# Masked keys on GpSimd: four pieces behind both products instead of two around one

## What is computed

```python
qkv = win @ qkv_w + qkv_b
q, k, v = jnp.split(qkv, 3, axis=-1)
q = to_heads(q) * dh ** (-0.5)
attn = jnp.einsum('bhnd,bhmd->bhnm', q, k)
attn = attn + bias                      # and the mask of shifted windows
attn = jax.nn.softmax(attn, axis=-1)
out = jnp.einsum('bhnm,bhmd->bhnd', attn, v)
out = out @ proj_w + proj_b
```

## Time and profile before

| | |
|---|---|
| median of 3 runs | 8296.84 us (8291.62 to 8297.04) |
| the profiled execution | 8299.7 us, of which the span of the trace is 8298.0 us |
| TensorE's matmuls busy | 94% of the span |
| ScalarE, VectorE busy | 75%, 73% |
| GpSimd busy | 43% |
| mean granted TensorE clock | 0.976 of full speed |

### The profile page before, as it was taken

The page is one execution under the profiler, slowest core; times in us unless marked ns, Lnnn a source line. Parts: engine busy times, 40 slices in busy tenths (PEclk is TensorE's granted clock), DMA queues, the critical chain, the costliest instruction groups (busy, mean ns, idle before and its releaser), DMA issues.

```text
span 8298.0 us, 213285 instructions
## 1 busy us (share of the span) xinstructions
PE 7781.9 (94%) x76732; PEld 4632.0 (56%) x76732; DVE 6095.1 (73%) x12339; ACT 6242.5 (75%) x11905; POOL 3585.1 (43%) x2453
## 2 busy tenths in 40 slices
PE   6899999999999999999999999999999999999997
PEld 4655555555555555555555555555555555555554
DVE  6377777777777777777777777777777777777774
ACT  0288878887888888778878878888787888787781
POOL 4244444444444444444444444444444444444440
PEclk9999999999999999999999999999999999999996
DMA  7000000000000000000000000000000000000006
GB/s 218 9 20 20 19 19 19 19 21 19 19 19 19 21 18 19 19 20 19 19 19 20 19 19 19 19 20 19 21 19 19 19 21 19 19 19 21 19 16 205
DMA packets 286131, 236.84 MB, mean 29 GB/s; under 512 B 41564, under 2 KB 280670, under 8 KB 284766
## 3 DMA queue, kind: packets, MB, share of 16 engines
q1 hardware_dynamic: 240944, 179.42, 8.1%
q10 hardware_dynamic: 35886, 19.97, 0.8%
q0 software_dynamic: 8192, 22.49, 0.8%
HBM read 112.56 MB, written 109.18 MB: 27 GB/s over the span
## 4 chain that ended last, share of the span: by engine, by line
issue 53%; POOL 30%; PE 10%; ACT 3%; DMA 3%; DVE 1%; POOLq 1%; SPq 0%; ACTq 0%; DVEq 0%
POOL E L411 19%; POOL Kbd L420 11%; PE bank L867 1%; PE bank L900 1%; DMA cm<-xT 1%; DMA xT<-cm 1%; PE bank L885 1%; PE bank L926 1%; PE bank L957 1%; PE bank L848 1%; PE bank L849 1%; PE bank L1017 1%; PE bank L943 1%; ACT E L472 0%; PE bank L962 0%
## 5 line engine op out<-in xcount | busy, mean ns | idle before, releaser
L411 POOL TENSOR_TENSOR E<-E,rs 113x588 f32<-113x588 f32 x1536 | 1819.2, 1184 | 3379.0 <-DVE rs L701 3379.0
L670 DVE TENSOR_TENSOR S<-bank,bias 113x294 f32<-113x294 f32 x3072 | 1412.5, 460 | 1428.9 <-PE bank L885 1364.8
L420 POOL TENSOR_TENSOR Kbd<-KT,headmask 112x1176 f32<-112x1176 f32 x768 | 1701.8, 2216 | 1042.6 <-ACT KT L478 1042.6
L867 PE MATMUL bank<-ident,E 113*113 113x113 f32 x9216 | 1620.3, 285 | 289.1 <-ACT ET L446 160.4
L867 PEld LDWEIGHTS bank<-ident,E 113*113 113x113 f32 x9216 | 1232.6, 180 | 1086.5 <-issue 540.8
L446 ACT ACTIVATE ET<-bank 113x339 f32<-113x339 f32 x3072 | 1367.7, 445 | 489.2 <-PE bank L867 471.3
L900 PEld LDWEIGHTS bank<-ET,V 113*48 113x48 f32 x36864 | 1005.5, 126 | 781.5 <-ACT ET L446 485.5
L695 DVE TENSOR_REDUCE sm<-E 113x12 f32<-113x588 f32 x1536 | 1163.8, 758 | 328.2 <-ACT E L472 328.2
L678 DVE TENSOR_REDUCE mx<-S 113x12 f32<-113x588 f32 x1536 | 1172.2, 763 | 39.6
L684 DVE TENSOR_TENSOR S<-S,mx 113x588 f32<-113x588 f32 x1536 | 1168.5, 761 | 0.0
L900 PE MATMUL bank<-ET,V 113*48 113x49 f32 x36864 | 1152.5, 212 | 10.3 <-issue 9.8
(11 more groups left out here) (88 smaller groups left out, 9136.9 us busy)
## 6 DMA issues: line engine op xcount, KB each, us to landing
xin<-xT SPq DMA_DIRECT2D x384, 98.0 KB, 2.0
xT<-xout SPq DMA_DIRECT2D x384, 98.0 KB, 1.8
xin<-xT SPq DMA_DIRECT2D x384, 73.5 KB, 2.0
xT<-xout SPq DMA_DIRECT2D x384, 73.5 KB, 1.8
xT<-cm POOLq DMA_DIRECT2D x128, 171.5 KB, 3.6
cm<-xT SPq DMA_DIRECT2D x128, 171.5 KB, 3.6
tm<-in_x SPq DMA_DIRECT2D x128, 147.0 KB
out<-tm ACTq DMA_DIRECT2D x128, 147.0 KB
```

What stands on the lines that cost most here:

```text
L411: pool.tensor_tensor(e, e, r, ALU.mult).then_inc(norm_done, 1)
L420: pool.tensor_tensor(Kbd[:, j.mod(2), p0:p0 + P // 2], k, m, ALU.mult).then_inc(kbd_done, 1)
L670: dve.tensor_tensor(strided(S[:, p, 0, 0:1], [[1, HN]]), pS[p % 2][0:M2, 0:HN], bi, ALU.add)\
L867: last = pe.transpose(pT[0:M2, k * M2:(k + 1) * M2], strided(E[:, j.mod(2), p, 2 * k, 0:1], [[1, M2]]), ident[0:M2, 0:M2])
```

## The change

GpSimd now makes Kbd in four pieces of two windows (112 x 588 elements each) instead of two of four windows (112 x 1176), and all of them after product 1. `kbd_done` rises four times a step. TensorE waits for the piece of each pair of windows instead of for a half at p = 0 and p = 4. ScalarE waits, before it overwrites KT, for the last piece of the step before.

```diff
-            def spread_k(j, half):
-
-                if half == 0:
+            def spread_k(j, quarter):
+
+                if quarter == 0:
                     pool.wait_ge(kT_done, gv(j, 1, 1))
-                p0 = half * P // 2
-                k = strided(KT[:, p0, 0:1], [[N, P // 2], [0, HEADS], [1, N]])
-                m = strided(headmask[:, 0:1], [[0, P // 2], [1, HEADS], [0, N]])
-                pool.tensor_tensor(Kbd[:, j.mod(2), p0:p0 + P // 2], k, m, ALU.mult).then_inc(kbd_done, 1)
+                p0 = 2 * quarter
+                k = strided(KT[:, p0, 0:1], [[N, 2], [0, HEADS], [1, N]])
+                m = strided(headmask[:, 0:1], [[0, 2], [1, HEADS], [0, N]])
+                pool.tensor_tensor(Kbd[:, j.mod(2), p0:p0 + 2], k, m, ALU.mult).then_inc(kbd_done, 1)
...
                 if b:
                     norm(b, 0)
-                if a:
-                    spread_k(a, 0)
                 if b:
                     norm(b, 1)
                 if a:
-                    spread_k(a, 1)
+                    for quarter in range(4):
+                        spread_k(a, quarter)
...
                 act.wait_ge(k_mm, gv(j, 1, 1))
+                if not j.before(1):
+                    act.wait_ge(kbd_done, gv(j, 4, 0))
                 act.activation(flat(KT), pA0[0:R, 0:TOK], ACT.Identity, bias=cols[:, t, BK:BK + 1]).then_inc(kT_done, 1)
...
-                if p % (P // 2) == 0:
-                    pe.wait_ge(kbd_done, gv(j, 2, 1 + 2 * p // P))
+                pe.wait_ge(kbd_done, gv(j, 4, 1 + p // 2))
```

## The result

| | before | changed |
|---|---|---|
| median of 9 runs | 8298.36 us (8291.62 to 8306.60) | 8321.85 us (8317.10 to 8327.99) |
| the profiled execution, its span | 8299.7 us, 8298.0 us | 8319.77 us, 8318.1 us |
| mean granted TensorE clock | 0.976 | 0.973 |

The ratio is 1.0028 [1.0017, 1.0038]: slower by 23.5 us. That is above the 0.2% that I had called measurable and outside my range, which ended at 8318.

What follows compares the result with a forecast made beforehand. The prediction took alternating ScalarE and TensorE stretches, a 19.68 us step repeated 384 times, to bound the kernel. Its five terms were all 0, giving 8297 us, no change, with a range of 8278 to 8318 us.

Steps and rivals of the forecast that it cites:

- The bound: ScalarE's and TensorE's stretches close the 19.68 us step, repeated 384 times; POOL and VectorE matter only if late.
- Part 1: On POOL, product 1 goes ahead of the keys and starts 1.79 us earlier; nobody waits for it: worth 0.
- Part 2: On POOL, four key pieces replace two halves at 1.14 us each; the last ends 0.64 us later.
- Part 3: TensorE's need for the pieces: piece 0 is 1.68 us in time, the others are asked for later: worth 0.
- Part 4: POOL-VectorE port: last piece overlaps the subtraction 0.08 us, 0.13 is free, 0.41 more spare: worth 0, upper end 1344 us.
- Rival 1: POOL-VectorE port wait outgrows the slack: 154 us slower per 0.1 us a piece above 1.255 us; chance 0.10.
- Part 5: Added kbd_done waits on TensorE and ScalarE, and ScalarE's register instruction, are already fulfilled or hidden: 0.
- The sum: All five terms are 0, so the whole kernel was forecast at 8297 us, no change.
- rival 3: TensorE's loop-pass ends, 6.0 or 4.7 us each, shift with the code: -27 to +27 us; chance 0.10, half slower.
- Rivals 2 and 4: TensorE waits for POOL: up to 173 us faster, chance 0.05; ScalarE's register instruction delays its path: +12 to +31 us, 0.03.

## Why the prediction was wrong, by its own steps

- **The bound** (ScalarE's and TensorE's stretches, POOL and VectorE in neither): right. Only a GpSimd operation that overlaps VectorE's subtraction by 0.72 us, where the change makes it 0.09 (medians), moved the period.
- **Part 1** (product 1 earlier, worth 0): right, it starts 0.08 us after its reciprocal, and no stop of TensorE got shorter.
- **Part 2** (1.14 us a piece): right. The four pieces span 4.60 us, forecast 4 x 1.14 + 0.04.
- **Part 3** (who needs them, 0): right; GpSimd's part alone gave 1.0002.
- **Part 4** (port, 0): the value for this change was right, with 0.14 us of overlap (0.08 forecast) and 0.78 us for L685. The model beyond it was wrong. Its upper end of 1344 us assumed that VectorE waits until GpSimd has nothing left; with pieces of 2.13 us the one in flight at 4037.89 would end at 4039.80, a wait of 1.78, and (1.78 - 0.41) x 384 = 526 us would pass, an estimate. Rival 1's price of 154 us for each 0.1 us stands only where the last piece is the one in flight, and there the extra product of 294 elements cost 0.10 us a step for the 0.18 of this sum. The extra product of 588 elements gave 1.0029, no more than the changed kernel's 1.0028. In both runs the wait was at most what was left of one operation.
- **Part 5** (added waits, 0): right for what the waits do, and this is where the loss still came in. I counted the two instructions ahead of the transposes inside the loop and left out the straight code: the three loops begin 10, 22 and 34 places later. By themselves they cost nothing; they move the loops.
- **The sum** is the step that failed. It had no term for the pass ends. It named them as rival 3, with the right place, the right size (6.0 or 4.7 us a return) and even the right sentence ("by where the code lies"), but gave the slower half a chance of 0.05 and took nothing of it into the sum. The missing term is -4 us in phase 1 and +23 in phase 2, +19.4 in all.
- **Much of it could have been worked out**, given the weights of the count and the period of 256. The trace of before has returns of 5.89 us at distance 67, with second stops, and of 4.64 at 81, without; and the built program of the changed kernel tells that phase 0 goes to 57, phase 1 from 202 to 180 and phase 2 from 81 to 47. Phase 2 at no less than phase 0's price is 14 x 1.25 = +17.5 us at once. That trace alone shows a single place with a second stop, though; the weights came out of the later runs.
- **Rivals 2 and 4** (TensorE waiting for POOL; ScalarE's register instruction): neither showed. The period grew by 0.005 us, 2 us over all steps, where rival 4 needs 0.03 to 0.08 each; and the ratio of the changed kernel with 70 instructions, 0.9980, equals the 0.9983 of before with 85 within their intervals.

What stays open. Why the stops lie at 196 to 198 and not at a multiple of 256 isn't shown; whatever runs ahead of the program would move that number; nor do these runs show that the period is 256. The 0.3 to 0.5 us between returns at 202 to 208 and at the other large distances are explained in part: the first stop lasts 3.2 to 3.35 us there (medians of a phase), 2.9 to 3.1 at the others, and why isn't known. Nor is it known what decides between the short and the long stretch at the lower clock behind a single stop. The 0.08 us a step that the loop absorbed of the port wait have no explanation either.

## What to carry to other kernels

- Where an engine in a hardware loop stops at the return and shows "issue", compare the passes of different loops with the same body. If they differ, count the place of each loop's first instruction before trusting any result below half a per cent: an edit that only adds instructions somewhere ahead can cost or give that much. Compare two versions with the place equalised, as pads of fulfilled waits allow. Check that the place is out of play in every loop: 60 pads made this kernel 0.8% slower, 85 made it 0.2% faster.
- First make the returns few. Here one cost about 5.2 us, and a body four times as long gave 2.2%, more than the whole span of place effects (8289 to 8370 us).
- VectorE, which shares a port with GpSimd here, waited for the operation in flight and not for the queue behind it, so short pieces on the other engine bound the wait.

## What the hardware showed that I had not expected

- Two stops per loop return on TensorE: 2.5 to 3.5 us at the return, and 0.3 to 2.6 us more when the place of the second stop (4292 or 17350) is reached sooner than about 2.7 us into the pass. The row says "issue" in the midst of one group of matmuls.
- The stretch at 1.2 GHz around a return came in lengths: about 3.4 or 6.8 us with one stop (86 and 109 of 196 returns), 6.8 or 10.2 in the phases with second stops (138 of 140). The longer one costs some 1.25 us more.
- 70 instructions more made the kernel 32 us faster (8321.85 to 8289.58, on two chips; the ratios to before on the same chip, 1.0028 and 0.9980, make it about 40).
- GpSimd and VectorE take turns at their port one operation at a time: VectorE got in between two queued GpSimd operations, and the second then took 1.71 us for 1.18.
